# A two-layer network in one kernel: weights ordered on chip, keys first, tokens placed earlier, last expert's downs first

## The reference, cut to what matters

```python
x = x + attention(layernorm(x), Wq, Wkv, Wout)     # 16 heads, 16 wide keys, 64 wide values
x = x + ffn(layernorm(x), w_gate, w_up, w_down)    # silu(gate) * up, 384 hidden, int weights
x = x + mixing(layernorm(x), W, U, mixes, Wk, Wv, Wr, Wo)
x = x + experts(layernorm(x), router_w, router_b, w1, b1, w2, b2)
# attention: q, k, v l2-normed by head; attn = relu(q k^T)^2; out = tanh_norm(attn v); out @ Wout
# mixing (RWKV): K, V, R from x and x of the token before; aa, bb, pp run over the 256 tokens of a
#   sequence (pp a running maximum); y = (e1*aa + e2*v) / (e1*bb + e2); out = (sigmoid(R) * y) @ Wo
# experts: 8, top 2 of a softmax; a token's slot is its rank (cumsum) in the expert, 320 at most;
#   gelu(buf @ w1 + b1) @ w2 + b2, gathered back and weighted by the gates
```

## Time and profile before

| | us |
|---|---|
| median of 3 runs | 460.76 |
| the three runs | 459.39, 460.76, 463.52 |
| profiled execution, its own time | 462.12 |
| profiled execution, span from first to last instruction | 460.5 |
| mean granted TensorE clock | 0.887 of full speed |

### The profile page before, as it was taken

How to read it: one execution, slowest core, us unless ns; L and a number is a source line. 1 busy time by engine, 2 the same in 40 slices (tenths; PEclk the granted TensorE clock), 3 DMA queues, 4 the chain that set the end, 5 groups by cost and what they waited for, 6 DMA issues and landing times. The chain is left out here.

```text
span 460.5 us, 6760 instructions
## 1 busy us (share of the span) xinstructions
PE 363.8 (79%) x2371; PEld 220.6 (48%) x2371; DVE 273.6 (59%) x622; ACT 234.9 (51%) x414; POOL 179.9 (39%) x342
## 2 busy tenths in 40 slices
PE   0869798899999999997799888868573571799940
PEld 0434445466474746564365463544331430478740
DVE  4655474775848585766556657794879820043233
ACT  1757577567757584953353428883656300333400
POOL 3041726437273735786342105000006776015550
PEclk9969999899999999997789999997876566799985
DMA  8600000000000000000000005700000110423337
GB/s 155 164 1 0 2 0 2 0 1 1 2 1 0 1 1 3 1 1 0 1 1 0 2 0 162 302 0 1 1 0 32 56 31 6 128 80 122 126 121 210
DMA packets 26481, 19.81 MB, mean 43 GB/s; under 512 B 9490, under 2 KB 23203, under 8 KB 26064
## 3 DMA queue, kind: packets, MB, share of 16 engines
q1 hardware_dynamic: 21216, 14.92, 11.1%
q0 software_dynamic: 1824, 2.89, 2.0%
q10 hardware_dynamic: 3408, 1.57, 1.3%
HBM read 12.12 MB, written 8.32 MB: 44 GB/s over the span
## 5 line engine op out<-in xcount | busy, mean ns | idle before, releaser
L601 DVE TENSOR_TENSOR at_attn<-at_sim,at_attn 128x1024 f32<-128x1024 f32 x64 | 75.2, 1216 | 20.5 <-ACT at_attn L455 20.3
L455 ACT ACTIVATE at_attn<-at_sim 128x1024 f32<-128x1024 f32 x64 | 62.2, 1026 | 45.2 <-PE at_sim L239 44.8
L256 PE MATMUL at_av<-at_attn,at_v_raw 128*64 128x256 f32 x512 | 69.4, 418 | 0.8 <-DVE at_v_raw L592 0.8
L1238 POOL DMA_INDIRECT mo_slots<-ro_rows,ro_put x32 | 32.4, 1012 | 69.4 <-DVE ro_put L1664 60.2
L732 POOL TENSOR_TENSOR at_osq<-at_ob 128x512 f32<-128x512 f32 x32 | 34.4, 1076 | 61.8 <-ACT at_ob L463 61.2
L239 PE MATMUL at_sim<-at_q,at_k 32*128 32x256 f32 x512 | 47.1, 436 | 12.0 <-DVE at_attn L601 10.1
L256 PEld LDWEIGHTS at_av<-at_attn,at_v_raw 128*64 128x64 f32 x512 | 36.7, 148 | 29.0 <-issue 15.3
L592 DVE TENSOR_TENSOR at_v_raw<-at_v_raw,at_key_factor 128x1024 f32<-128x1024 f32 x16 | 20.7, 1301 | 38.0 <-POOL at_key_factor L752 38.0
L239 PEld LDWEIGHTS at_sim<-at_q,at_k 32*128 32x128 f32 x512 | 27.8, 198 | 29.3 <-DVE at_attn L601 16.0
L205 PE MATMUL at_misc<-at_w_v,at_xnT 128*128 128x512 f32 x64 | 34.5, 638 | 0.7 <-ACT at_sq_v L433 0.6
L1839 POOL DMA_INDIRECT mo_answers<-mo_ye,mo_to x18 | 17.4, 968 | 36.6 <-DVE mo_ye L1958 34.5
(11 more groups left out here) (274 smaller groups left out, 660.0 us busy)
## 6 DMA issues: line engine op xcount, KB each, us to landing
mo_w<-in_L_ffn_w SPq DMA_DIRECT2D x16, 256.0 KB, 3.2
mo_answers<-mo_zero SPq DMA_DIRECT2D x2, 1024.0 KB, 12.9
mo_got<-mo_answers SPq DMA_DIRECT2D x6, 256.0 KB, 3.7
mo_slots<-mo_empty SPq DMA_DIRECT2D x1, 1440.0 KB, 10.3
mo_xe<-mo_slots SPq DMA_DIRECT2D x5, 288.0 KB, 4.8
x_res<-in_L_attn_tokens SPq DMA_DIRECT2D x4, 256.0 KB, 3.5
at_w_v<-in_L_attn_Wkv ACTq DMA_DIRECT2D x1, 512.0 KB, 6.0
at_w_out<-in_L_attn_Wout SPq DMA_DIRECT2D x1, 512.0 KB, 5.4
```

Source lines behind the costliest of these rows:

```text
L256: last = mm(av[e * DV:(e + 1) * DV, half * T:(half + 1) * T], v_raw[b % 2][:, j, h * DV:(h + 1) * DV], attn[(2 * Q + half) % 4][:, e, j, : ...
L455: nc.scalar.activation(attn[n % 4][:, :, :, :].rearrange("p e j t -> p e (j t)"), sim[half][:, :, :], ACT.Relu).then_inc(relu_ready, 1)
L601: v.tensor_tensor(r, sim[half][:, :, :], r, ALU.mult).then_inc(attn_ready, 1)
L1238: g.indirect_dma_start(moe.slots, bass.IndirectOffsetOnAxis(put[:, k, t:t + 1], 0), rows[:, t, :], None, bounds_check=SLOTS - 1, oob_is_er ...
```

## The change

In the head: Wq and Wkv are loaded whole, from ScalarE's queue; four ScalarE copies bring the Q and K columns into order, and V's columns are read where they lie (64 of every 80). Batch 0's x is a transfer of its own (two tiles), the others follow; VectorE takes statistics of two tiles, normalises batch 0, takes the other 14, normalises batch 1. Three matmuls on zeros stand first on TensorE. The table of ScalarE's functions is loaded first. The first inverse norms are done on VectorE (`first_factors`), and no longer on GpSimd.

In the mixing block: K is projected ahead of V in chunks 2 and 3; `up(3, 2)` goes to the output bank `yw`; `inverse_deviations` stands between the scans of `states`; `normalize_w` comes ahead of `gate` on ScalarE; chunks 0 and 1 are chosen, counted and placed ahead of `total(2)`; `subtract_max(3)` comes ahead of `output(2)`; the part of `count` that needs only earlier tiles is a step of its own (`count_before`); `place(1)` comes ahead of `inverse_deviations(3)`; two pairs of matmuls that nobody reads are added, and eight at the end are taken away.

In the experts: two such matmuls and the first transposes come ahead of the wait for b1, instead of three behind it; and `down(6)` comes ahead of `up(7)`.

```diff
--- before.py
+++ after.py
...
+        w_q, w_kv = sb("w_q", [P, HEADS * DK]), sb("w_kv", [P, HEADS * (DK + DV)])
         w_qk = sb("w_qk", [P, 2, GROUPS_QK, P])
-        w_v = sb("w_v", [P, V])
+        w_v = w_kv[:, :].rearrange("p (h d) -> p h d", h=HEADS)[:, :, DK:DK + DV]
+        idle = sb("idle", [P, 512])
         w_out = sb("w_out", [P, PAIRS, P])
...
+        X_PARTS = (0, TPB), (TPB, 3 * TPB), (3 * TPB, 5 * TPB), (5 * TPB, TILES)
...
         def _(sp):
-            sp.dma_start(xr[:, 0:Q4, :], x_tiles[:, 0:Q4, :]).then_inc(x_loaded[0], 16)
+            def load_x(n):
+                first, end = X_PARTS[n]
+                sp.dma_start(xr[:, first:end, :], x_tiles[:, first:end, :]).then_inc(x_loaded[n], 16)
+            load_x(0)
             sp.dma_start(ident[:, :], ident_in).then_inc(ident_loaded, 16)
-            for s, src in enumerate((Wq.rearrange("p (h d) -> p h d", h=HEADS), kv_view[:, :, 0:DK])):
-                for g in range(GROUPS_QK):
-                    for p in range(2):
-                        at = 8 * g + 4 * p
-                        sp.dma_start(w_qk[:, s, g, :].rearrange("p (h e d) -> p h e d", e=2, d=DK)[:, :, p, :],
-                                     src[:, at:at + 4, :]).then_inc(w_qk_loaded, 16)
-            for n in range(1, 4):
-                sp.dma_start(xr[:, n * Q4:(n + 1) * Q4, :], x_tiles[:, n * Q4:(n + 1) * Q4, :]).then_inc(x_loaded[n], 16)
+            for n in range(1, len(X_PARTS)):
+                load_x(n)
             sp.dma_start(w_out[:, :, :], Wout.rearrange("(s p) n -> p s n", p=P)).then_inc(w_out_loaded, 16)
...
                 t, half = j // 2, j % 2
-                mm(bank[:, :], xnT[b % 2][:, t * P:(t + 1) * P], w_v[:, half * 512:(half + 1) * 512],
+                mm(bank[:, :], xnT[b % 2][:, t * P:(t + 1) * P], w_v[:, half * 8:(half + 1) * 8, :],
                    start=True, stop=True).then_inc(v_done, 1)
...
+            pe.wait_ge(idle_ready, 1)
+            for _ in range(3):
+                mm(av[:, :], idle[:, 0:P], idle[:, :], start=True, stop=True)
             pe.wait_ge(ident_loaded, 16)
             transpose_x(0, m0)
-            pe.wait_ge(w_qk_loaded, 16 * 8)
+            pe.wait_ge(w_qk_ready, GROUPS_QK)
             project_qk(0, 0, m1)
+            pe.wait_ge(w_qk_ready, 2 * GROUPS_QK)
             project_qk(0, 1, m2)
-            pe.wait_ge(w_v_loaded, 16)
+            pe.wait_ge(w_kv_loaded, 16)
             project_v(0, 0, m0)
...
         def _(act):
-            act.dma_start(w_v[:, :].rearrange("p (h d) -> p h d", h=HEADS), kv_view[:, :, DK:DK + DV]).then_inc(w_v_loaded, 16)
+            act.dma_start(w_q[:, :], Wq).then_inc(w_q_loaded, 16)
+            act.dma_start(w_kv[:, :], Wkv).then_inc(w_kv_loaded, 16)
+            nc.scalar.preload_act_table_set("exp_and_others")
...
+            for s, (w, loaded, width) in enumerate(((w_q, w_q_loaded, DK), (w_kv, w_kv_loaded, DK + DV))):
+                act.wait_ge(loaded, 16)
+                columns = w[:, :].rearrange("p (g e h d) -> p g h e d", e=2, h=4, d=width)
+                for n in range(GROUPS_QK):
+                    nc.scalar.copy(w_qk[:, s, n, :].rearrange("p (h e d) -> p h e d", h=4, e=2),
+                                   columns[:, n, :, :, 0:DK]).then_inc(w_qk_ready, 1)
+            copy_xT(0, m0)
             act.wait_ge(picks_loaded, 48)
-            copy_xT(0, m0)
             keep_qk(0, 0, m1)
...
-            x_stats(0, Q4)
+            def first_factors():
+                dve.wait_ge(vsum_ready, 2)
+                at = slice(QK.start, VS.stop)
+                x, y, a = zx[:, at], zy[:, at], za[:, at]
+                link.wait()
+                dve.wait_ge(ns_read, 1)
+                link(v.tensor_scalar(x, z[:, at], NORM_FLOOR, None, ALU.max))
+                rsqrt(nc, link, y, x, a, y.bitcast(I32), x.bitcast(I32))
...
+                                ALU.mult).then_inc(key_factor_ready, 1)
+                link(v.tensor_tensor(r4[0][:, :, :], r[:, :, 0, :], r[:, :, 0, :], ALU.mult))
+            x_stats(0, TPB)
             normalize_x(0)
+            x_stats(TPB, TILES)
             normalize_x(1)
-            x_stats(Q4, TILES)
             read_norms(1, None, 0, m1)
...
             reduce_v(0, 1)
+            first_factors()
             square(0)
...
             link = Chain(pool, pool_chain)
+            g.memset(idle[:, :], 0.0).then_inc(idle_ready, 1)
             for dst, src in ((halves[:, :], halves_in), (pick[:, :, :], pick_in), (sel_f32[:, :, :], sel_in)):
...
-            inverse_norms(1, None, 0)
             for b in range(BATCH):
...
                     pe.wait_ge(xf_added, c)
-                pe.wait_ge(ahead.h_ready, HB * c + max(k - 1, 0))
+                if bank is yw_bank:
+                    pe.wait_ge(xw_added, c - 2)
+                else:
+                    pe.wait_ge(ahead.h_ready, HB * c + max(k - 1, 0))
                 mm(bank[:, :], ahead.ffn.w_gu[:, 1, k * P:(k + 1) * P], ahead.xfT[c % 2][:, :], start=True,
...
+            def count_before(r):
+                first, end = ROUTED[r]
+                n = end - first
+                pe.wait_ge(shifted, r + 1)
+                pe.wait_ge(mask_ready, r)
+                place = route_bank(r)
+                mm(place, one_row[0:1, :], slot_base[0:1, :].unsqueeze(1).to_broadcast([1, n, EXPERTS]), start=True, stop=False)
+                for t in range(first):
+                    mm(place, ones[:, :], mask[:, t:t + 1, :].to_broadcast([P, n, EXPERTS]), start=False, stop=False)
...
                 place = route_bank(r)
-                mm(place, one_row[0:1, :], slot_base[0:1, :].unsqueeze(1).to_broadcast([1, n, EXPERTS]), start=True, stop=False)
                 mm(place, tri[:, :], mask[:, first:end, :], start=False, stop=False)
-                for t in range(end - 1):
-                    at = max(t - first + 1, 0)
+                for t in range(first, end - 1):
+                    at = t - first + 1
                     last = mm(place[:, at:n, :], ones[:, :], mask[:, t:t + 1, :].to_broadcast([P, n - at, EXPERTS]),
...
+            def stay_busy(n):
+                for _ in range(n):
+                    mm(yw_bank[:, :], moe.ident[:, :], ahead.xfT[0][:, :], start=True, stop=True)
...
             up(3, 1, yf_bank)
+            up(3, 2, yw_bank)
             transpose_w(2)
+            project_k(2)
             project_v(2)
-            project_k(2)
-            up(3, 2, u_bank)
             subtract_max(2)
...
             logit(1)
+            stay_busy(2)
             transpose_w(3)
+            project_k(3)
+            count_before(0)
+            count(0)
             project_v(3)
-            project_k(3)
+            subtract_max(3)
             output(2)
-            subtract_max(3)
-            count(0)
...
             logit(2)
+            pe.wait_ge(totals, LAST + 1)
+            stay_busy(2)
+            count_before(1)
             output(3)
...
             logit(3)
+            count_before(2)
             count(2)
-            pe.wait_ge(routed, len(ROUTED))
-            for _ in range(8):
-                mm(d_bank[:, :], moe.ident[:, :], ahead.xfT[0][:, :], start=True, stop=True)
...
             seeds(0)
+            ahead.normalize_w(act, 2)
             gate(1)
-            ahead.normalize_w(act, 2)
             ahead.copy_w(act, 2, xt[:, :])
...
             seeds(1)
-            gate(2)
             ahead.normalize_w(act, 3)
             ahead.copy_w(act, 3, xt[:, :])
+            exp_logits(0)
+            normalize_m(1)
+            gate(2)
             invert(2)
             open_gate(2)
-            exp_logits(0)
-            normalize_m(1)
             weigh(3, 0)
...
-            def states(c):
+            def states(c, between=None):
...
                     done.then_inc(sums_ready, 1)
+                    if n == 0 and between:
+                        between()
...
-            states(1)
-            inverse_deviations(0)
+            states(1, lambda: inverse_deviations(0))
             total(1)
...
             ahead.hidden(dve, 3, 1, yf_bank[:, :])
-            ahead.hidden(dve, 3, 2, u_bank[:, :])
+            ahead.hidden(dve, 3, 2, yw_bank[:, :])
             running_max(2)
...
             dve.wait_ge(consts, 10)
-            states(2)
-            inverse_deviations(1)
-            total(2)
-            gate(2)
+            states(2, lambda: inverse_deviations(1))
             shift(0)
-            finish(2)
-            running_max(3)
             choose(0)
...
             place(0)
+            total(2)
+            gate(2)
+            running_max(3)
+            finish(2)
             add_output(2)
-            states(3)
-            inverse_deviations(2)
+            states(3, lambda: inverse_deviations(2))
             total(3)
...
             softmax(1)
+            place(1)
             inverse_deviations(3)
-            place(1)
             shift(2)
...
             mm = nc.tensor.matmul
```

(23 more changed lines are left out.)

9 lines of the change are left out of this document (7 added, 2 removed).

## The result

The changed kernel takes 445.75 us (median of 4, 443.06 to 452.95) against 460.07 us for the kernel before (458.66 to 463.52); the ratio is 0.9645, 95% interval 0.9605 to 0.9685, so 14.5 to 18 us less. The forecast was 450.2, and the low end of its range 445.5. Measured a second time the change gave a median of 449.27 (442.07 to 449.63); the median of all eight executions is 448.2. Every ratio leaves out the slow executions, those over 1.5% above the fastest of their kernel (452.95 here, three of the four of the second measurement, two of the six with the head alone, and one each at 547.68, 553.28 and 552.33 us with keys first only, with early placing only and of the kernel before), while the medians keep them, so that a kernel with a wide spread shows a smaller gain in its median than in its ratio.

A forecast was written before the change was run, and what follows sets the result against it. Bound by chained waits: place(0) sets the first of 32 back-to-back GpSimd scatters before the experts. Gains 2.0+6.8+0.9+0.9 = 10.6 take the profiled span from 460.5 to 451.5, the median from 460.76 to 450.2; range 445.5 to 456.5.

The forecast's parts named there:

- the head's term: Kernel's head: projections 1.4 us earlier, TensorE's clock 0.3, first norms on VectorE 0.3; gain 2.0, bounds 0 and 4.
- untouched: Attention loop, about 31 to 240 us: the change leaves it alone; no gain or loss was summed for it.
- mixing: Mixing block: keys first and early placing of chunks 0 and 1 bring scatter 17 forward; gain 6.8 us, bounds 5.0 and 8.6.
- First scatter: Mixing block, GpSimd: first scatter of routed rows goes at 334.5, 13.4 us earlier, after place(0) ends near 333.5.
- hole on GpSimd: Mixing block: GpSimd waits 5 to 8 us before scatter 17, which needs place(1); forecast wrong if this is absent.
- Opening: Start of the experts: fewer idle matmuls, earlier slot transposes, up(0) perhaps at half clock; gain 0.9 us, bounds -1.0 and 2.1.
- Last expert: End of the experts: down(6) ahead of up(7) lets GpSimd's last scatters go earlier; gain 0.9 us, bounds 0.4 and 1.2.
- (a): Rival: full clock through K and V of chunk 2 and the openings; 445.2 us, more likely 446 to 447; chance 0.15.
- (b): Rival: lower clock in all these places, nothing from the head; gain 4.5, at 456.3 us; chance 0.21 with (e).
- (e): Rival: mixing block's placing not moved in effect, count(0) or exp_logits(0) late by 7 us or more; chance 0.21 with (b).
- (c): Rival: mixing block's first 16 scatters slow beside VectorE, 2.3 us apart; block loses 1.7, 458.7 us; chance 0.04.
- (d): Rival: V's weights read inside Wkv halve the moving operand's speed; 464 us; chance 0.05 with other losses that size.

The follow-up runs named there:

- keys first only: Kernel before with K projected ahead of V in chunk 2, up(3, 2) in the output bank, normalize_w(2) ahead of gate(1): 458.61 us, ratio 0.9952.
- early placing only: Kernel before with chunks 0 and 1 placed early, K and V order and inverse_deviations(0) as before: 460.39 us, ratio 0.9970.
- the seven at the start: Changed kernel with idle matmuls in loop and mixing block, seven instead of three ahead of the first transposes: 441.68 us, ratio 0.9588 to before.

## Why the prediction was off

The step that failed is the head's term, "Head: 1.4+0.3+0.3 = 2.0, bounds 0 and 4", with the premise that the loop of attention "is untouched". Its own mechanism was mis-sized by about 1.4: `scale_v` came 3.4 earlier. The Wkv load was down at about 6.0 and not 8.5 (it landed 4.8 us after its issue, though it carries more bytes than the 512 KB of the earlier trace rows), so the projections came 2.5 earlier and not 1.4; and first factors took 3.8, so that the norms gave 0.7 and not 0.3.

The larger part was not in the forecast at all. It reads TensorE's clock in the mixing block, at 0.61, and takes the like for the openings, but reads no window of the loop. There the clock was 0.70, 0.50 and 0.52 in the three windows from 24 to 36 us, 0.57 at 56 to 60, 0.62 at 84 to 88, and between 212 and 236 it was 0.66, 0.50, 0.98, 0.87, 0.50 and 0.78. A loop of unchanged code need not keep its length. In the first profile of the change A shrank by 9.0, of which 3.4 is the head's steps; the other 5.6 is the loop, 205.36 for 211.02.

How much of the 5.6 belongs to the change and how much to chance? Seven executions with the old head have loops from 208.77 to 212.08 (middle one 209.34); three with the new one have 205.36, 208.87 and 213.02. The last is longer than any with the old head, in an execution of the whole change whose `scale_v` came earliest of the three (25.32), and its clock is 0.50 at 24 to 28, 52 to 56, 80 to 84 and 212 to 220 us. So the new head does not prevent the falls, and in the middle values the gain of A, 4.6, is hardly more than that of `scale_v`, 3.75. The 5.6 of the first profile is luck as far as these traces go. One sign speaks for a share of the change: its best executions are better than the head's steps explain. The head alone reached 451.33 us, and none of some 65 executions of the kernel before was under 458.66. How the head would do that, by shorter waits or by moving them, is not shown. Shown is the clock's price in the loop, some 7 us (idle matmuls alone gave it back), and with it a few falls more or less account for most of the spread from 442 to 453.

By parts: **mixing**, forecast 6.8 (5.0 to 8.6); measured 6.1 in the first profile, 6.1 to 6.6 as a whole time. Right, with its halves 4.0 (forecast 4.0) and 3.7 (2.8) in B, each good to some 1.5. First scatter forecast 13.4 earlier, was 12.9 (58.02 for 70.96); hole on GpSimd forecast 5 to 8, was 6.22; scatter 17 forecast 0.95 behind the cast, was 354.41-353.46 = 0.95. **Opening**, 0.9 (-1.0 to 2.1): 1.8 with the up-projection at full clock, -0.4 in the first profile with it at half (C 0.3 shorter, 0.7 of that the last expert's); the range holds both. **Last expert**, 0.9 (0.4 to 1.2): 0.7. The chain still ended in the last scatter:

```profile
431.11 4.06 DMA mo_answers<-mo_ye_last,mo_to
```

Of the rivals, (a) had the time, 445.2, by luck, since its reason did not hold: in the first profile K and V of chunk 2 took 5.37 us in all where full clock gives 3.6, and the first up-projection ran at half clock. The full clock came in the attention loop. (b) and (e) are out by the first scatter. (c) happened in small: 5 of the first 16 scatters took 1.10 us or more, the first 1.91, and the hole of 6.22 covers all of it; the 17th to 32nd are back to back. By the rule cited beside it (the Trainium skill, SBUF — State Buffer, the "DVE blocks DMA" trap), as the forecast applied it, every scatter beside such VectorE work would wait. The trace shows 5 of 16, and no run here shows whether it was that lock which held them. (d) is out: the median V instruction takes 592 ns both before and after, read out of Wkv with its gaps.

Two slips in the working change nothing: 8.5, two copies of 0.3 and 0.4 make 9.5 and not 9.7, and the GELUs' times stand in the earlier trace rows, not the earlier trace rows.

With the median of all eight executions, 448.2, the forecast of 450.2 is 2 off, of which the head's size is 1.4. But the sum had no term for the loop, and so the range, down to 445.5, had no room for executions at 442 to 444.

## What to carry to other kernels

Before summing a change's parts, read the granted clock over the whole span, the unchanged loops too: in a loop with short waits the same instructions may run at 2.4 GHz in one execution and at 1.2 in the next. Where TensorE waits briefly and often, matmuls of zeros in a free bank can be worth more than a reordering: here 6.9 us for 23 of them, and the changed kernel with them spread over 3.2 us in place of 11. They must end before the work that they stand ahead of is ready, or they cost what they give, as the seven at the start did. Two versions should be compared by several executions or with the clock held full in both, and a part's gain in one trace should be held against how far that part moves in traces where nobody touched it.

## What was unexpected of the hardware

Two executions of the same instructions, alike in granted clock to 0.01 for 224 us, then differed (0.50 and 1.00 in 228 to 232 us). Two plain loads of 128 and 640 KB landed sooner than one of 512 KB had among small ones (4.8 us for the larger, 6.0 before). Behind waits of 1.88 and 0.43 us at a slot's end twelve score matmuls took 1.99 us, where full clock gives 1.13.
